# One fused layer (splat attention, norm, sparse FFN, norm): thirteen turned output sets are weighed by ScalarE and GpSimd instead of VectorE

## What is computed

```python
q, k, v = heads(x @ Wq.T), heads(x @ Wk.T), heads(x @ Wv.T)      # 16 heads of 16
scores = q @ k.T / sqrt(16)                                      # causal
std = softmax(mask(scores)) @ v                                  # "plain"
gsa = softmax(mask(scores + 0.3 * splat_terms(q, k))) @ v        # "guided"
blend = min(0.03, sigmoid(gsa_strength) * 0.15)
x = layernorm(x + (1 - blend) * std @ Wo.T + blend * gsa @ Wo.T)
h = silu(x @ w_gate) * (x @ w_up); h = keep_2_largest_of_every_4(h)
x = layernorm(x + h @ w_down)
```

## Time and profile before

| | |
|---|---|
| median of 3 runs | 396.21 us (395.86 to 396.52) |
| profiled execution, span from first to last instruction | 396.0 us |
| PE busy | 372.8 us (94%) |
| DVE busy | 303.9 us (77%) |
| ACT busy | 229.6 us (58%) |
| POOL busy | 125.7 us (32%) |
| one pair of heads in the loop | 30.4 us |

### The profile page before, as it was taken

How to read it: one execution, slowest core, us unless ns; L and a number is a source line. 1 busy time by engine, 2 the same in 40 slices (tenths; PEclk the granted TensorE clock), 3 DMA queues, 4 the chain that set the end, 5 groups by cost and what they waited for, 6 DMA issues and landing times.

```text
span 396.0 us, 6714 instructions
## 1 busy us (share of the span) xinstructions
PE 372.8 (94%) x2234; PEld 255.1 (64%) x2234; DVE 303.9 (77%) x900; ACT 229.6 (58%) x451; POOL 125.7 (32%) x173
## 2 busy tenths in 40 slices
PE   6998999999999999999999999999889899999995
PEld 6666568565665665675664664764435488888884
DVE  2766999997897897897898898795024367999955
ACT  3965443675675685684784774775766836443100
POOL 8377657403303303302302312284395200000000
PEclk9998999999999999999999999999989999999999
DMA  6062540450540540540550558000000000000003
GB/s 201 22 105 47 81 81 4 67 95 10 88 70 4 87 75 6 89 73 4 82 82 3 80 86 319 4 2 0 5 0 2 0 2 0 0 2 0 2 0 106
DMA packets 12907, 19.70 MB, mean 50 GB/s; under 512 B 5492, under 2 KB 8564, under 8 KB 12872
## 3 DMA queue, kind: packets, MB, share of 16 engines
q1 hardware_dynamic: 10328, 18.18, 22.9%
q0 software_dynamic: 1536, 1.07, 1.6%
q10 hardware_dynamic: 1008, 0.02, 0.1%
HBM read 5.26 MB, written 1.05 MB: 16 GB/s over the span
## 4 chain that ended last, share of the span: by engine, by line
PE 69%; DVE 19%; ACT 6%; issue 2%; DMA 2%; SPq 1%; POOL 0%; DVEq 0%; ACTq 0%
PE ps L937 17%; PE ps L963 14%; PE ps L902 13%; DVE ps L1270 11%; PE ps L863 7%; PE ps L765 5%; PE ps L767 5%; PE ps L766 5%; DVE mpart L1263 2%; PE ps L924 2%; ACT pr L713 2%; DMA x_sb<-_attn_hidden_states_dram 2%; DVE mpart L1270 2%; PE ps L847 1%; PE ps L827 1%
## 5 line engine op out<-in xcount | busy, mean ns | idle before, releaser
L713 ACT ACTIVATE pr<-ps 128x512 f32<-128x512 f32 (+2 forms) x320 | 154.8, 571 | 75.8 <-PE ps L963 74.7
L1270 DVE CUSTOM_DVE_ANT_0 ps<-ps,causal 128x512 f32<-128x512 f32 (+3 forms) x256 | 144.9, 615 | 19.0 <-PE ps L902 18.2
L902 PE MATMUL ps<-k_st,q_st 65*128 65x512 f32 (+5 forms) x384 | 120.9, 369 | 3.5 <-DVE mpart L1270 2.8
L963 PE MATMUL ps<-q_st,k_st 67*128 67x512 f32 (+7 forms) x384 | 122.2, 363 | 0.3 <-ACT pr L713 0.3
L963 PEld LDWEIGHTS ps<-q_st,k_st 67*128 67x128 f32 (+1 forms) x384 | 68.3, 191 | 39.4 <-issue 21.5
L902 PEld LDWEIGHTS ps<-k_st,q_st 115*128 115x128 f32 (+1 forms) x384 | 67.9, 190 | 25.8 <-DVE mpart L1270 15.7
L937 PE MATMUL ps<-pr,vx 128*32 128x512 f32 (+3 forms) x768 | 74.1, 497 | 1.9 <-ACT o_sb L699 1.0
L558 POOL TENSOR_SCALAR_AFFINE_SELECT pr<-pr 128x512 f32<-128x512 f32 x64 | 40.5, 634 | 87.7 <-ACT pr L713 87.3
L1263 DVE TENSOR_REDUCE mpart<-ps 128x1 f32<-128x384 f32 (+2 forms) x96 | 54.9, 596 | 7.3 <-PE ps L902 7.0
L937 PEld LDWEIGHTS ps<-pr,vx 128*32 128x32 f32 x768 | 19.4, 109 | 32.1 <-issue 17.4
L1270 DVE DVE_READ_ACCUMULATOR2_ANT mpart<- 128x1 f32 x256 | 36.0, 141 | 0.0
(11 more groups left out here) (190 smaller groups left out, 497.5 us busy)
## 6 DMA issues: line engine op xcount, KB each, us to landing
q_st<-base_hiq SPq DMA_DIRECT2D x28, 64.0 KB
k_st<-base_hik SPq DMA_DIRECT2D x28, 64.0 KB
q_st<-feat_hiq SPq DMA_DIRECT2D x28, 64.0 KB
k_st<-feat_hik SPq DMA_DIRECT2D x28, 64.0 KB
x_sb<-_attn_hidden_states_dram SPq DMA_DIRECT2D x4, 256.0 KB, 6.5
raw<-in_L_ffn_w_gate_dram SPq DMA_DIRECT2D x1, 1024.0 KB, 4.8
raw<-in_L_ffn_w_up_dram SPq DMA_DIRECT2D x1, 1024.0 KB, 7.0
wd<-in_L_ffn_w_down_dram SPq DMA_DIRECT2D x1, 1024.0 KB, 9.1
```

The source lines that it names most:

```text
L713: act.activation(pr[:, s % NP, 2 * hh + vs[0]:2 * hh + vs[-1] + 1, d:BANK], src, ACT.Exp, scale=SCALE).then_inc(exp_done, 1)
L902: mm = pe.matmul(ps[:, slot, at:at + n], q_st[b][0:rows, hh, i * P:(i + 1) * P], k_st[b][0:rows, hh, first:first + n], start=(v == v0), st ...
L963: mm = pe.matmul(ps[:, bank, j * width:(j + 1) * width], k_st[b][0:rows, hh, kt * P:(kt + 1) * P], q_st[b][0:rows, hh, q:q + width], start ...
L1270: ins = dve.tensor_tensor_reduce(out=ps[:, slot, at:at + n], in0=ps[:, slot, at:at + n], in1=causal[:, BANK - n:BANK], scale=1.0, scalar=- ...
```

## The change

For a set whose place in the ring is ahead of the last ("turn_max", 7), DVE now takes only the reciprocal. ACT copies the 128x256 outputs from the ring bank into `otmp` right behind the first exp of the following step. POOL forms `rw` from `rec` and `blend`, multiplies `otmp` by `rw` in place, and adds the halves as before. By the planner's lists these are thirteen sets, (0, 0) to (6, 0): seven ahead of the rows, six in mid-pair. The last three keep the old form.

```diff
+    carried = [it for it in ring if it[0] == "turn_out" and ring_at[it] < ring_at[("turn_max", PAIRS - 1)]]
+        inverted, carried_over, weighed = sem("inverted"), sem("carried_over"), sem("weighed")
@@ GpSimd, blend_sum
-                pool.wait_ge(ring_free, ring_at[("turn_out", p, g)] + 1)
+                it = ("turn_out", p, g)
+                pool.wait_ge(ring_free, ring_at[it] + 1)
+                if it in carried:
+                    e = carried.index(it)
+                    pool.tensor_tensor(rw[:], rec[:], blend[:].rearrange("p a v -> p (a v)"), ALU.mult).then_inc(weighed, 1)
+                    pool.wait_ge(weighed, e + 1)
+                    pool.wait_ge(carried_over, e + 1)
+                    outs = otmp[:].rearrange("p t h v d -> p (t h v) d")
+                    pool.tensor_tensor(outs, outs, rw[:].unsqueeze(2).broadcast_to([P, 16, HD]), ALU.mult).then_inc(scaled, 1)
+                    pool.wait_ge(scaled, G + e + 1)
@@ ScalarE
+            def carry(it):
+                e, r = carried.index(it), ring_at[it]
+                act.wait_ge(ring_free, r + 1)
+                if e >= 1:
+                    act.wait_ge(attn_done, e)
+                act.activation(otmp[:].rearrange("p t h v d -> p (t h v) d"),
+                               ps[:, ring_bank[r], :].rearrange("p (a e) -> p a e", e=32)[:, :, 0:HD],
+                               ACT.Copy).then_inc(carried_over, 1)
...
+                    if t == 0 and s > 0:
+                        for it in at_step[s - 1]:
+                            if it in carried:
+                                carry(it)
@@ TensorE, item
                     pe.wait_ge(ring_free, latest(ring_bank, r, slot))
+                    if ring[latest(ring_bank, r, slot) - 1] in carried:
+                        pe.wait_ge(carried_over, carried.index(ring[latest(ring_bank, r, slot) - 1]) + 1)
@@ VectorE
+                    if it in carried:
+                        if e >= 1:
+                            dve.wait_ge(weighed, e)
+                        dve.reciprocal(rec[:].unsqueeze(2), sums_v[:, :, HD:HD + 1]).then_inc(ring_free, 1)
+                        r += 1
+                        continue
+                    dve.wait_ge(weighed, len(carried))
```

## The result

The changed kernel takes 410.04 us (median of 4 runs, 408.94 to 413.68) against 396.07 us (4 runs, 395.86 to 396.52): ratio 1.0374, 95% interval 1.0323 to 1.0424. The profiled execution has a span of 407.2 us against 396.0. The direction was right and the size wrong: 403.5 had been forecast, 406.8 at most. The times of all kernels are medians, and runs more than 1.5% above the fastest of their kernel are left out: two of e2 (416.5 and 417.3 us), one each of p1 (421.0) and d1 (424.2), and the profiled one of p2 (702.3). The ratios are those on record with their intervals; the quotient of two medians differs from them by up to 0.4%.

The account below looks back on a forecast made before the run. Path held by PE's values and scores matmuls (75%) and DVE's maxima (about 18%). Relief 0, copy 1.7 and collision 5.6 make 7.3 us on 396.0, 403.3, and 0.2 for the median: 403.5 us; range 399.3 to 406.8.

Parts of the forecast that it names:

- DVE's relief: 0.67 us off DVE in each of thirteen sets, 8.7 us, worth nothing; rival that it counts, chance 0.03.
- The copy: ACT's copy behind the first exp delays later exps 0.29 us in six mid-pair sets, 1.7 us; ahead of rows 0.
- The collision: POOL's work holds up DVE's two-SBUF-operand rows operations, 0.80 us in seven sets, 5.6 us; rival without it, chance 0.12.
- three cases: Delay of DVE's rows by the POOL operations they meet: 0.46, 0.80 or 1.14 us; chances 0.23, 0.35, 0.27.
- the middle one: DVE's rows wait for the weighing, then the addition: 0.80 us in each of seven sets, 403.5 us; chance 0.35.
- The third: DVE's rows wait for the next mask too: 1.14 us in each of seven sets, 405.9 us; chance 0.27.
- the doubt whether the mask: Whether POOL's mask, under way at the last rows operation, blocks it too, making the delay 1.14 us, not 0.80.
- The weighing: POOL's multiplication of the 128x256 outputs, taken as 0.77 us, starting 0.07 us behind ACT's copy.
- the lowest case: First rows operation slips ahead of the weighing, later ones wait for weighing and addition: 0.46 us, 401.1 us; chance 0.23.
- the upper end of the range: Whole kernel at 406.8 us, with all three collisions and the copy costing 0.40 us.
- The port rule: GpSimd contends with DVE instructions of two SBUF inputs; if only with 2-port ones, the weighing is free, total 398.

Follow-up runs that it names:

- e2: Against the kernel before, the change made only for the seven sets ahead of the rows: 408.40 us, ratio 1.0327.
- p1: The kernel before plus two idle GpSimd multiplications of 128x256 in SBUF beside VectorE's rows, nothing handed over: 409.63 us, ratio 1.0333.
- d1: The kernel before plus three idle VectorE multiplications of 128x256 ahead of the rows of pairs 1 to 7: 417.37 us, ratio 1.0577.
- p2: The kernel before plus four GpSimd memsets of 128x256 beside VectorE's rows, which read nothing: 396.79 us, ratio 1.0020; its profiled execution took 702.26.
- s3: The kernel before with the sets ahead of the rows changed, GpSimd's part two steps later, TensorE turning these sets after the values: 393.23 us, ratio 0.9897.
- p3: The same kernel as p2 (four GpSimd memsets beside the rows of the kernel before), run again for its trace: 397.24 us, a single run.
- s1: The kernel before, only with TensorE turning the sets ahead of the rows after the values of the step: 397.36 us, ratio 1.0049.

## Why the prediction was wrong, point by point

- **DVE's relief is worth nothing: right.** The idle time behind the reciprocal is 1.36 us, the forecast figure to the hundredth. With the turned sets moved, in s3, the same relief counts.
- **The copy: right.** 0.24 us in mid-pair against 0.29; 6 x 0.24 = 1.4 us against 1.7.
- **The collision: the mechanism right, the size too small.** I had priced three cases, 0.46, 0.80 and 1.14 us, and took the middle one. The third came, 1.15 us in each of seven pairs: 8.0 us against 5.6. The step that failed is the doubt whether the mask, which reads one operand, would block like the two-operand operations. It did, L1283 took 0.59 us under it. The weighing itself took 0.62 us, not 0.77; that changed nothing, since POOL also started later (0.14 us behind the copy, not 0.07), still just ahead of DVE. Two sums of the prediction are off without consequence: by its own times the lowest case comes to 0.34 us (L1256 would end at 121.97 in place of 121.63), not 0.46, and the upper end of the range to 396.2 + 8.0 + 2.4 = 406.6, not 406.8.
- **The clock: missing, and this took the time out of the range.** With 1.15 and 0.24 the sum is 9.5 us, 405.7, which the range still held. The step that failed is that PE's longer wait was counted as a wait and nothing more. In the profiled execution it brought three falls of the clock, 1.6 us each, 4.9 us. With the shorter opening that makes 9.5 + 4.9 - 2.9 = 11.5, against the 11.2 measured. The median of the four runs lies 14.0 above that of before; the two slower runs had a lower mean clock than the profiled one, which fits more falls, but no trace shows them. The trace of before had such a stretch: in pair 7 PE waits 1.50 us for ACT at 292.52, and from 292.9 us it is granted half its clock. I read that row for DVE and not for PE. It would not have given the number of falls: the same trace has a wait of 1.04 us at 284.53 with none behind it.

```profile
292.52 0.77 PE L924 MATMUL ps<-ident,o_sb 128*128 128x128 f32 x4 [1.50 <-ACT o_sb L699]
...
292.00:294.00 2.00, 1.48 (x7) 1.26 (x7) 0.64 (x2) 1.11 (x3) 1.92 (x2) 0.72 0.00 0
294.00:296.00 2.00, 2.00 (x10) 0.20 (x8) 1.22 (x2) 1.33 (x3) 1.92 (x2) 0.50 0.00 0
```

- **The port rule.** Of the two statements of the Trainium skill that were weighed, that of the GPSIMD Engine Reference, Key points, which names DVE instructions with two SBUF inputs as well, held (p1, 31.3 us a pair), though not beside every GpSimd instruction: a memset did not hold the tensor_tensors of p3. By the narrower one of Advanced Engine Details and Errata, Mode Summary, the tensor_tensors of p1 would have kept 0.17 to 0.19 us; they took up to 0.61.

## What to carry to other kernels

Work that leaves a busy engine is worth nothing where that engine idles right behind it; look at the row behind, not at the engine's share. Before GpSimd gets elementwise work, list the VectorE operations with two SBUF operands that can fall beside it, and place it where there are none: the same work on thirteen sets costs 14 us, and 1.5 when GpSimd does seven of them two steps later. And where TensorE is made to wait longer in a nearly full loop, price falls of its clock with the wait: here waits of 0.8 us (s1) and 1.3 us were followed by one in two or three cases of six, at 1.5 to 1.6 us each.

## What was not expected of the hardware

- A wait of TensorE of 1.3 us (busy 0.68 of 2 us) can be followed by 3.4 us at 1.2 GHz in place of 2.4, which costs this loop 1.6 us, more than the wait itself.
- POOL's affine_select, with one operand in SBUF, holds up a DVE tensor_tensor as fully as a two-operand multiplication does (0.59 us against 0.19). A memset does not; only a cast beside it took 0.08 us more.
- The kernel before varies between 392.6 and 396.3 us of span with the number of such falls, so two kernels are best compared by pairs with the full clock, and only then by medians.
